# Expert layer of a fused transformer block on one Trainium2 core: the second product with the weight block stationary, its output turned back by transposes

## The reference, cut to what matters

```python
gates, idx = jax.lax.top_k(probs.T, cap)                       # 8 experts x 660 tokens
xe = xn[idx]                                                   # (8, 660, 256)
hmid = jnp.einsum('ech,efh->ecf', xe, fc1_w) + fc1_b[:, None, :]   # 1024 hidden
hmid = jax.nn.gelu(hmid, approximate=False)
ye = jnp.einsum('ecf,ehf->ech', hmid, fc2_w) + fc2_b[:, None, :]   # back to 256
weighted = (ye * gates[..., None]).reshape(-1, h)
out = jnp.zeros((T, h), x.dtype).at[flat_idx].add(weighted)
gate_sums = jnp.zeros((T, 1), x.dtype).at[flat_idx].add(gates.reshape(-1, 1))
out = out / jnp.maximum(gate_sums, 1e-09)
```

## Time and profile before

| | |
|---|---|
| times, us | 927.32, 929.59, 934.68; median 929.59 |
| profiled execution, us | 929.86, its span 928.0 |
| busy, share of the span | PE 84%, PEld 77%, DVE 68%, ACT 34%, POOL 31% |
| fc1 (L1016), whole kernel | 768 matmuls, 128×330 |
| fc2 (L1031), whole kernel | 1152 matmuls, 128×256 |
| transposes of the gathered tokens (L998) | 96 |
| mean granted TensorE clock | 0.924 of full |

### The profile page before, as it was taken

One profiled execution on the slowest core, in us unless ns is written; L12 is line 12 of the kernel. 1 busy time (PEld: TensorE's weight loads), 2 busy tenths in 40 slices (PEclk: granted clock), 3 DMA queues, 4 the chain that ended last, 5 costly groups with the idle time before them and its releaser, 6 DMA issues. The chain is left out here.

```text
span 928.0 us, 19977 instructions
## 1 busy us (share of the span) xinstructions
PE 782.6 (84%) x7394; PEld 714.4 (77%) x7394; DVE 635.5 (68%) x1551; ACT 319.9 (34%) x668; POOL 288.1 (31%) x312
## 2 busy tenths in 40 slices
PE   4899999999999999999998311159999999999997
PEld 2678888888888888888886211149999899999997
DVE  1337786787776777867765566766877878778662
ACT  0204333433333433333332200007346273462560
POOL 3011212221222212222211520030743836538434
PEclk8899999999999999999998655559999999999999
DMA  9946646656456555466461640010532525424122
GB/s 288 267 72 83 81 82 105 106 84 93 82 85 113 94 89 82 85 98 109 83 96 31 192 153 0 0 31 1 105 121 31 137 56 106 124 24 100 30 34 31
DMA packets 81643, 83.15 MB, mean 90 GB/s; under 512 B 36249, under 2 KB 75911, under 8 KB 81212
## 3 DMA queue, kind: packets, MB, share of 16 engines
q1 hardware_dynamic: 68948, 67.82, 36.8%
q0 software_dynamic: 11584, 10.96, 7.5%
q10 hardware_dynamic: 1032, 3.33, 1.1%
HBM read 35.52 MB, written 16.22 MB: 56 GB/s over the span
## 5 line engine op out<-in xcount | busy, mean ns | idle before, releaser
L609 ACT ACTIVATE r_arena<-ps_all 126x660 f32<-126x660 f32 x128 | 92.2, 720 | 107.1 <-PE ps_all L789 107.1
L528 POOL DMA_INDIRECT xe<-xn_rows,r_arena x48 | 69.5, 1448 | 190.4 <-DVE r_arena L1401 106.3
L1139 DVE TENSOR_REDUCE mx<-ps_all 128x4 f32<-128x504 f32 (+1 forms) x160 | 104.5, 667 | 16.3 <-PE ps_all L765 16.1
L1150 DVE RECIPROCAL r_arena<-ps_all 128x165 f32<-128x165 f32 x64 | 76.1, 1189 | 57.0 <-PE ps_all L804 57.0
L1031 PE MATMUL ps_all<-W_hi,hT_hi 128*110 128x256 f32 x384 | 109.4, 285 | 0.0
L1031 PE MATMUL ps_all<-W_hi,hT_lo 128*110 128x256 f32 x384 | 108.1, 282 | 0.0
L1031 PE MATMUL ps_all<-W_lo,hT_hi 128*110 128x256 f32 x384 | 108.0, 281 | 0.0
L789 PE MATMUL ps_all<-Qp,Kp 98*126 98x166 f32 x512 | 102.6, 315 | 0.0
L541 POOL DMA_INDIRECT out<-r_arena x48 | 88.4, 1841 | 38.2 <-issue 35.5
L1439 DVE TENSOR_TENSOR hT_lo<-r_arena,hT_hi 128x330 fp32r<-128x330 f32 x128 | 63.3, 501 | 41.1 <-ACT r_arena L673 39.9
L765 PE MATMUL ps_all<-Kp,Qp 96*65 96x56 f32 (+1 forms) x512 | 90.4, 293 | 0.0
(11 more groups left out here) (161 smaller groups left out, 1745.0 us busy)
## 6 DMA issues: line engine op xcount, KB each, us to landing
H<-w SPq DMA_DIRECT2D x16, 1024.0 KB
Qp<-q_hi SPq DMA_DIRECT2D x64, 166.0 KB, 3.9
Kp<-k_hi SPq DMA_DIRECT2D x128, 63.0 KB, 4.2
Qp<-q_lo SPq DMA_DIRECT2D x32, 166.0 KB, 4.6
out<-H SPq DMA_DIRECT2D x16, 330.0 KB
xn_rows<-r_arena SPq DMA_DIRECT2D x16, 330.0 KB
Kp<-k_lo SPq DMA_DIRECT2D x64, 63.0 KB, 4.0
H<-h SPq DMA_DIRECT2D x1, 3360.0 KB, 23.4
```

The lines of the kernel that those rows point to most:

```text
L528: pool.indirect_dma_start(xe[0:A, a, :], None, xn_rows, bass.IndirectOffsetOnAxis(tok[0:A, u, a:a + 1], 0), bounds_check=NTOK - 1).then_in ...
L609: act.activation(PT[0:S, g, :, :].rearrange("p (k h) t -> p k h t", k=2), pair[:, :, :, 0:T], ACT.Exp, scale=float(HD) ** -0.5).then_inc(e ...
L1139: dve.tensor_reduce(dst, src, AX.X, ALU.max).then_inc(max_ready, 1)
L1150: dve.reciprocal(rS[:, c, :], bank(2 + c)[:, T:2 * T]).then_inc(rs_sum, 1)
```

## The change

The second product is turned over. A 128×128 block of W2 is stationary and 330 tokens move, so one expert has four pieces (two halves of tokens × two blocks of 128 output values, here called quarters) of 24 matmuls each, and the result has output values on partitions. ACT adds the bias, now a column per partition, while it takes each quarter out of PSUM into `yS` (`evacuate`). PE turns `yS` back with 12 transposes per expert (`output_rows`), six for each half; the last six are put into the next expert, behind its first block of fc1. `weigh` is one DVE operation on the transposed tile instead of two. The expert loops of PE and ACT are written out instead of looped, and eight small broadcast loads of the bias on SP fall away. POOL's list is as before.

```diff
-            def fc2(e, tiles):
-                for a in tiles:
-                    if not (isinstance(e, int) and e == 0 and a < 2):
-                        pe.wait_ge(y_ready, NA * e + a - 1)
-                    rows = slice(a * A, (a + 1) * A)
-                    terms = [(h, w, f) for f in range(KFF)
-                             for h, w in ((hT_hi, W2_hi), (hT_hi, W2_lo), (hT_lo, W2_hi))]
...
-                        mm = pe.matmul(bank(4 + a % 2)[0:A, 0:D], h[:, f, rows], w[:, f, :],
+            def fc2(e, quarters):
+                for q in quarters:
+                    j, c = q // 2, q % 2
+                    if j == 1:
+                        pe.wait_ge(y_evac, 4 * e + c + 1)
+                    elif e >= 1:
+                        pe.wait_ge(y_ready, NA * (e - 1) + 5 + c)
+                    cols = slice(j * HALF, (j + 1) * HALF)
...
+                        mm = pe.matmul(bank(4 + c)[:, 0:HALF], w[:, f, c * 128:(c + 1) * 128], h[:, f, cols],
                                        start=(i == 0), stop=(i == len(terms) - 1))
                     mm.then_inc(fc2_done, 1)
+            def output_rows(e, tiles):
+                for a in tiles:
+                    at_bank, at_col = y_place[a]
+                    if a % 3 == 0:
+                        pe.wait_ge(y_evac, 4 * e + 2 * (a // 3) + 2)
+                    for c in range(KD):
+                        mm = pe.transpose(bank(at_bank)[0:A, at_col + c * 128:at_col + (c + 1) * 128],
+                                          yS[:, c, a * A:(a + 1) * A], ident)
+                    mm.then_inc(yt_done, 1)
...
+            for e in range(NE):
+                split = KFF if e == 0 else SV_AT
+                fc1(e, range(0, 1))
+                if e >= 1:
+                    output_rows(e - 1, range(3, NA))
+                fc1(e, range(1, split))
+                if e + 1 < NE:
+                    slot_values(e + 1, True)
+                fc1(e, range(split, KFF))
+                fc2(e, range(0, 2))
+                if e + 1 < NE:
+                    expert_transposes(e + 1, range(0, 2))
+                fc2(e, range(2, 3))
+                output_rows(e, range(0, 3))
+                if e + 1 < NE:
+                    expert_transposes(e + 1, range(2, 4))
+                fc2(e, range(3, 4))
+            output_rows(NE - 1, range(3, NA))
```

On ACT and DVE:

```diff
+            def evacuate(e, quarters):
+                for q in quarters:
+                    j, c = q // 2, q % 2
+                    act.wait_ge(fc2_done, 4 * e + q + 1)
+                    if e >= 1 and c == 0:
+                        act.wait_ge(yt_done, NA * (e - 1) + 3 * j + 3)
+                    act.activation(yS[:, c, j * HALF:(j + 1) * HALF], bank(4 + c)[:, 0:HALF], ACT.Identity,
+                                   bias=b2_s[:, e, c:c + 1]).then_inc(y_evac, 1)
...
-                    dve.tensor_tensor(yt[0:A, a % 2, :], bank(4 + a % 2)[0:A, 0:D], b2_s[0:A, e, :], ALU.add)\
-                       .then_inc(y_chain, 1)
-                    dve.wait_ge(y_chain, NA * e + a + 1)
-                    dve.tensor_scalar(yw[0:A, a, :], yt[0:A, a % 2, :], wslot[0:A, u, a:a + 1], None, ALU.mult)\
-                       .then_inc(y_ready, 1)
+                    dve.tensor_scalar(yw[0:A, a, :], bank(at_bank)[0:A, at_col:at_col + D], wslot[0:A, u, a:a + 1],
+                                      None, ALU.mult).then_inc(y_ready, 1)
...
-                    hidden(e, u, seen, range(0, TOK_AT))
+                    hidden(e, u, seen, range(0, 1))
+                    weigh(e - 1, v, range(3, NA), e > 1)
+                    hidden(e, u, seen, range(1, TOK_AT))
                     tokens(e + 1, v, again)
                     hidden(e, u, seen, range(TOK_AT, KFF))
-                low_W1(e + 1, v, range(0, 1))
-                weigh(e, u, range(0, 1), again)
-                low_W1(e + 1, v, range(1, KD))
-                weigh(e, u, range(1, 2), again)
+                low_W1(e + 1, v)
                 if more:
                     one_hot_values(e + 2)
-                weigh(e, u, range(2, 3), again)
+                low_xeT(e + 1, range(0, 2))
                 if more:
                     one_hot_places(e + 2, range(0, 1))
-                weigh(e, u, range(3, 4), again)
-                low_xeT(e + 1, range(0, 2))
-                if more:
-                    one_hot_places(e + 2, range(1, 2))
-                weigh(e, u, range(4, 5), again)
+                weigh(e, u, range(0, 3), again)
                 low_xeT(e + 1, range(2, 4))
                 if more:
-                    one_hot_places(e + 2, range(2, NK))
-                weigh(e, u, range(5, NA), again)
+                    one_hot_places(e + 2, range(1, NK))
```

## The result

The changed kernel took 969.17 us in the median of four runs (967.26 to 972.32), the kernel before in the same comparison 931.94 (927.32 to 934.68): a ratio of 1.039, 95% interval 1.034 to 1.044. The change makes the kernel 3.9% slower. The prediction said 961, 3.4% slower.

A forecast was written before the change was run, and what follows sets the result against it. TensorE bounds the expert stage, with one wait for gathered tokens. Span 928.0 plus 4.0 (expert 0), 24.4 (experts 1 to 6) and 3.4 (last) gives 959.8, so about 961 us, 3.4% slower; range 947 to 972.

The forecast's parts named there:

- The bound: Expert stage: TensorE (PE) bounds, busy 35.53 of 37.12 us in expert 3; its rest is one wait for gathered tokens.
- the sum of PE's work: fc2 2.35 us less per expert, twelve output transposes 1.3 us more; PE's own work falls by 1.0 us.
- The term that decides: Gather, 12.6 us behind fc1's end, now covered by 7.3 us of fc2: PE waits 5.3 us per expert, formerly 1.6.
- The third term: Tail behind the last expert's fc2: three tiles come at once, 10.8 us instead of 6.4; last expert +3.4 us.
- R: Rival theory of the experiments: the turned product, with its evacuations and transposes back, costs something by itself; no chance given.
- the first case: Main case: gather wait and clock fall give 961 us, with bounds 957 to 969; chance 0.69.
- The clock behind each wait: PE falls to 1.2 GHz behind the token wait: 1.7 us in each of seven experts, bounds 1.43 to 2.4.
- The written-out loops: Expert loops of PE and ACT written out as Python loops: costed at nothing.
- The case that the clock stays: PE waits for the tokens but stays at 2.4 GHz: 12 us less, 949 us; chance 0.08.
- the quicker gather: POOL's gather is quicker, as for expert 1 (10.5 us): 13 us less, 948 us; chance 0.08.
- The fourth case: Last three tiles' scatters land 2 us late for `tokens`, delaying hidden blocks and fc1: 12 us more, 973; chance 0.07.

The follow-up runs named there:

- e12: e10 with the W2 weight loads held back until the gathered tokens have landed; ratio 0.993 to the kernel before.
- e11: e8 (old product) with the W2 weight loads held back until the gathered tokens have landed; ratio 0.990 to the kernel before.
- e1: Changed kernel with the transposes of the gathered tokens behind three quarters of fc2 instead of two, ACT's and DVE's lists following; ratio 1.024 to the kernel before.
- e5: e1 with all of DVE's one_hot_places moved behind low_xeT and weigh, out of the gather; ratio 1.012 to the kernel before.
- e2: Changed kernel with 28 useless matmuls of 330 columns per expert ahead of the transposes that wait for the gathered tokens; ratio 1.029 to the kernel before.
- e3: Changed kernel with SP's W2 weight loads held back until the next expert's gathered tokens have landed; ratio 1.036 to the kernel before.
- e4: Kernel before with only the expert loops of PE and ACT written out; ratio 1.005 to the kernel before.
- e6: e5 with the weights held back until the gather has landed and the token numbers one block of fc1 sooner; ratio 1.014 to the kernel before.
- e7: Changed kernel with the token numbers two blocks of fc1 sooner (SV_AT 2, TOK_AT 4); ratio 1.032 to the kernel before.
- e9: e7 with three slots for token numbers and gates instead of two, POOL's loop written out; ratio 1.021 to the kernel before.
- e10: e9 with the diffs of e1 and e5 (transposes behind three quarters, one_hot_places behind low_xeT); ratio 0.995 to the kernel before.
- e8: Kernel before with the token numbers two blocks of fc1 sooner (SV_AT 2, TOK_AT 4); ratio 0.991 to the kernel before.

## Why the prediction was right

**Right.** The bound, PE with one wait for the gathered tokens, was read rightly, and so was the sum of PE's work: 0.66 us for six transposes, 153 ns per fc2 matmul (3.65 us for 24), 1.0 us saved per expert; e12 against e11 shows 0.9 between experts. The term that decides was the place of the gather: 5.3 us of wait per expert were forecast, 5.7 measured. The clock fell in all seven waits. e1, e5 and e2 show that these two are the causes: moving the transposes behind the third quarter, with DVE's work out of the gather, takes 2.7 of 3.9% away (the wait and its falls of the clock together), filling the wait 1.0. The third term, the longer tail, is what is left of R.

**Sizes that were off.** All of them were too small: the predicted span was 959.8, the measured 969.3, and the measured median of 969.2 lies at the upper end of the first case's bounds of 957 to 969. The wait was 39.7 us instead of 37. In experts 1 to 4 the transposes came 2.4 to 3.9 us behind POOL's last issue and not 2.0, for the weights in the DMA queues; e3, which holds them back, has 1.8 to 2.1 there and 35.3 us of wait. I had taken only POOL's part of the gather from the rows. The clock behind each wait cost 2.07 us (14.4 / 7), where I took 1.7 between bounds of 1.43 and 2.4: 2.5 us more. PE worked at 0.50 for 3.1 us behind the wait of expert 1 and for 6.2 us behind that of expert 4, and the quarters took 4.49 and 5.89 us. The tail was 12.3 us and not 10.8. There the transposes waited 0.6 us for the evacuation and took 0.87 us, and the first of the last three scatters was issued at 960.73, some 3.7 us behind fc2 where I had 2.3. DVE had weighed its tile by about 958.7 (an estimate, a third of the way through its row below), but POOL was with the last scatter of the first half until 960.07, which the prediction had left out:

```profile
958.49 1.58 POOL L539 DMA_INDIRECT out<-r_arena  x1 [0.30 <-issue]
957.57 0.87 PE L1055 MATMUL ps_all<-cf,yS 128*110 128x128 f32 x6 [0.63 <-ACT yS L679]
958.26 1.27 DVE L1434 TENSOR_SCALAR r_arena<-ps_all,r_arena 110x256 f32<-110x256 f32 x3 [3.80 <-PE ps_all L1055]
960.73 1.58 POOL L539 DMA_INDIRECT out<-r_arena  x1 [0.66 <-issue]
```

The remaining 3.3 us lie ahead of the first expert.

**A term set at nothing.** The written-out loops cost 0.5% in e4, some 4 us, and nothing is what the prediction gave them. Whether they cost as much within the changed kernel was not tried.

**The rivals.** The case that the clock stays did not come, nor the quicker gather: its first two issues were 1.97 and 2.07 us as before. The fourth case, the scatters, stayed 1.3 us short of `tokens` by the estimate above and became a bound in e6 and e7.

The Trainium skill, "SBUF — State Buffer", section "Who interferes with whom", says that its own probe saw DVE's `tensor_copy` hold up the DMAs that GpSimd issues, but not `tensor_tensor`. Here the measurement differs: `one_hot_places` is a `tensor_tensor`, and the fifth issue beside it took 2.71 us in e1, against 1.08 in e5.

The Trainium skill, "TensorE: Matmul & The Clock Gate", section "HAM oscillation — how this bites in real kernels", describes a kernel whose waits for DMA put the array back to half rate tile after tile. This trace agrees, with seven waits of 4.5 to 7.0 us and seven falls to 0.50.

## What to carry to other kernels

When work on the bounding engine is made shorter or moved, look for what it was covering. Here 11.3 us of the old product had covered a gather, and the change put 7.3 us in front of the same wait to save 1.0. Then take the chain behind that wait apart into all of its parts: POOL's issues, the DMA queues and the scatters that let it start lay within a few us of each other, so that undoing one only brought up the next (e7, e9). Last, an operation that is turned so that its results come in fewer, larger pieces has its price in the last round, where nothing covers them; 4.8 us there is as much as five savings of 0.9.

## What the hardware did that I had not expected

**The clock fell without a wait.** In e12, PE was busy throughout, and still went to half clock behind `slot_values`, 48 matmuls of 30 bf16 columns (windows, columns as in the earlier trace rows):

```profile
774.00:776.00 2.00, 2.00 (x17) 1.75 (x15) 2.00 (x3) 1.39 (x4) 1.70 (x2) 1.00 0.59 59
776.00:778.00 2.00, 2.00 (x43) 2.00 (x42) 2.00 (x6) 1.01 (x3) 2.00 (x1) 1.00 0.47 54
778.00:780.00 2.00, 2.00 (x16) 2.00 (x15) 1.87 (x6) 0.00 (x0) 1.69 (x2) 0.64 0.32 24
780.00:782.00 2.00, 2.00 (x9) 2.00 (x8) 0.50 (x1) 1.07 (x3) 1.70 (x2) 0.51 0.34 41
```

The chain shows its price, 72 fc1 matmuls in 12.59 us instead of 11.07:

```profile
743.37 11.07 PE ps_all L1024 x72
...
778.43 12.59 PE ps_all L1024 x72
```

It happened in experts 4 and 6 of that profile, and at the same place in experts 3, 4 and 6 of e10. The small matmuls stand there two blocks earlier than in the kernel before, where they never did this. Their place alone is not the condition: in e8 and e11 they stand as early, with the old product, and the clock never fell there. Nothing was run to find what is.

**Useless work paid.** In e2, 30 us of matmuls that nobody reads made the changed kernel 1% faster, by holding the clock in six of seven waits.
